# A decoder layer on one core: PSUM banks chosen per job and tile at the two ends, another order of all work, and a quarter of the last experts' sums on ScalarE

## The reference

```python
# 1 causal self-attention, 16 heads of 8, polymax in place of a softmax
q, k, v = split(x @ W_attn, 3)
att = where(causal, q @ k.T / sqrt(8), -inf)
att = where(att > 0, att**2 + 1, where(att >= -100, -0.01 * att + 1, 0)) / 1000
x = layernorm(x + (att @ v) @ W_proj)
# 2 cross-attention, 16 heads of 64
q, k, v = x @ WQ, ctx @ WK, ctx @ WV
x = layernorm(x + softmax(q @ k.T / 8) @ v @ WO + bO)
# 3 16 experts, the 6 best kept by a router
probs = softmax(x @ router_w.T + router_b)
gate = top 6 of probs / (their sum + 1e-10), 0 elsewhere
out = sum over e of gate[:, e] * (x @ expert_w[e])
x = layernorm(x + out / max(sum(gate), 1e-10) + 1e-10 * sum(top_p))
```

## Time and profile before

| | |
|---|---|
| median of three runs | 1014.57 us (1012.44 to 1014.77) |
| profiled execution: its own time | 1011.26 us |
| its span, first to last instruction | 1009.5 us |
| mean granted clock of TensorE | 0.986 |
| PE busy | 955.2 us, 95% |
| PEld busy | 843.0 us, 84% |
| DVE busy | 890.6 us, 88% |
| ACT busy | 768.7 us, 76% |
| POOL busy | 434.3 us, 43% |
| instructions | 47204 |

### The profile page before, as it was taken

The page is one execution under the profiler, slowest core; times in us unless marked ns, Lnnn a source line. Parts: engine busy times, 40 slices in busy tenths (PEclk is TensorE's granted clock), DMA queues, the critical chain, the costliest instruction groups (busy, mean ns, idle before and its releaser), DMA issues.

```text
span 1009.5 us, 47204 instructions
## 1 busy us (share of the span) xinstructions
PE 955.2 (95%) x18136; PEld 843.0 (84%) x18136; DVE 890.6 (88%) x2824; ACT 768.7 (76%) x1606; POOL 434.3 (43%) x906
## 2 busy tenths in 40 slices
...
DMA packets 41882, 21.19 MB, mean 21 GB/s; under 512 B 18912, under 2 KB 40928, under 8 KB 41824
## 3 DMA queue, kind: packets, MB, share of 16 engines
...
...
## 4 chain that ended last, share of the span: by engine, by line
PE 66%; DVE 17%; issue 11%; ACT 3%; DVEq 1%; POOL 1%; DMA 0%; ACTq 0%; SPq 0%; POOLq 0%
PE ps L447 61%; DVE sums L888 4%; PE ps L572 4%; DVE allowed L852 3%; DVE p L864 2%; DVE stats L805 1%; DVE residual L888 1%; ACT prob L764 1%; DVE mv L811 1%; DVE best L911 1%; PE ps L595 1%; DVE ps L859 1%; DVEq L354 0%; ACT qm L636 0%; DVE left L920 0%
## 5 line engine op out<-in xcount | busy, mean ns | idle before, releaser
L888 DVE SCALAR_TENSOR_TENSOR sums<-ps,gate,sums 128x128 f32<-128x128 f32 x896 | 239.9, 340 | 18.5 <-PE ps L447 17.7
L996 POOL TENSOR_TENSOR p<-p,rowinv 128x1024 f32<-128x1024 f32 x64 | 121.8, 1904 | 219.1 <-DVE rowinv L841 219.0
L447 PE MATMUL ps<-wo_sb,oT 128*128 128x128 f32 x1024 | 127.5, 278 | 0.6 <-issue 0.6
L447 PEld LDWEIGHTS ps<-wo_sb,oT 128*128 128x128 f32 x1024 | 121.1, 192 | 5.4 <-issue 1.0
L636 ACT ACTIVATE v<-ps 128x512 f32<-128x512 f32 x128 | 76.3, 598 | 50.2 <-PE ps L447 45.2
L447 PE MATMUL ps<-ex_hi,x2T_hi 128*128 128x512 f32 x256 | 110.4, 431 | 3.3 <-POOL x2T_lo L978 3.1
L636 ACT ACTIVATE oT<-ps 128x512 f32<-128x512 f32 x128 | 69.6, 597 | 45.7 <-PE ps L447 45.1
L756 ACT ACTIVATE x<-residual,shift,rstd 128x128 f32<-128x128 f32 x192 | 83.7, 484 | 26.9 <-POOL shift L991 17.5
L447 PE MATMUL ps<-ex_lo,x2T_hi 128*128 128x512 f32 x256 | 101.7, 397 | 0.0
L447 PE MATMUL ps<-ex_hi,x2T_lo 128*128 128x512 f32 x256 | 101.5, 396 | 0.0
L852 DVE SCALAR_TENSOR_TENSOR allowed<-ps,const 128x512 f32<-128x512 f32 x128 | 87.1, 681 | 15.2 <-ACT relu L659 13.6
...
## 6 DMA issues: line engine op xcount, KB each, us to landing
...
```

The source lines that it names most:

```text
L447: return pe.matmul(o, l, r, start=start, stop=stop)
L888: done = V.scalar_tensor_tensor(after, ps(f"FF{4 * r + q}")[:, C * e:C * e + C], gate[:, r, 4 * q + e:4 * q + e + 1], before, ALU.mult, AL ...
L996: G.tensor_tensor(weights, weights, rowinv[:, r].unsqueeze(2).broadcast_to([P, H, T]), ALU.mult).then_inc(p2_ready, 1)
```

## The change

The diff does six things.

- `OTHER_BANK_FIRST` and `OTHER_BANK_LAST` name, for 205 entries of job and tile in head and tail, a bank other than that of `JOBS`. `banks_of` and `ps` take the tile.
- `JOBS` and `ORDER` hold another order and other banks for the loop. The turns run from 1 to 26, with a turn touching tiles from t - 1 to t + 4; FF3 and FF7 stand at t - 1.
- Head and tail orders are new. heads1, heads2 and heads0 take the pairs P3, P2 and P0, in this order, the first two right behind S1 of tile 0. `x_columns@2` stands ahead of `x_rows@1` on SP, `queries@1` ahead of `square3@0` on ACT.
- w_attn and the constants are issued on ACT's queue; on SP the order is WK, ctx of tile 0, WV, WQ.
- Four matmuls (`WARM`) on a tile of zeros run before PE's first wait.
- For the last three tiles (`SHARED`) `weigh3` is replaced. `scale3` on ACT multiplies the eight products of quarter 3 with their gates into SBUF, `gather3` on POOL adds them to one sum in two additions, and `join3` on DVE adds that to `sums`.

```diff
...
+SHARED = 3
+WARM = 4
...
+    ("FF7", "B0", -1), ("K2_0", "B1", 2), ("X2T", "B7", 0), ("PT0b", "B6", 1), ("Q", "B3", 4),
+    ("FF3", "B4", -1), ("K", "B5", 4), ("V", "B2", 4), ("Y", "B1", 3), ("S2_0", "P3", 2),
+    ("AC0", "P2", 1), ("S2_1", "P0", 2), ("LG", "B3", 0), ("PT1a", "B5", 1), ("PR", "B2", 3),
+    ("S1_0", "B7", 4), ("PT1b", "B3", 1), ("S1_1", "B4", 4), ("V2_0", "B5", 2), ("S1_2", "B6", 4),
+    ("S1_3", "B3", 4), ("AC1", "P0", 1), ("WO0", "B2", 1), ("WO1", "", 1), ("FF1", "B0", 0),
+    ("V2_3", "B1", 2), ("V2_1", "B7", 2), ("V2_2", "B2", 2), ("FF6", "B4", 0), ("PT0a", "B5", 2),
+    ("X1T", "B7", 3), ("FF4", "B1", 0), ("FF0", "B2", 0), ("Q2_0", "B7", 3), ("Q2_1", "B6", 3),
+    ("FF5", "B5", 0), ("FF2", "B3", 0), ("K2_1", "B7", 3), ("K2_3", "B6", 3), ("Q2_2", "B1", 3),
+    ("Q2_3", "B7", 3), ("K2_2", "B2", 3), ("heads0", "P0", None), ("heads1", "P0", None), ("heads2", "P0", None),
...
+        store@-1 context@4 x_rows@4 x_columns@5
...
+        mK2_3@2 mK2_0@2 mK2_2@2 mX2T@0 mPT0b@1 queries@4 kK@4 mV@4 mY@3 mAC0@1 norm3@-1 mPT1a@1 mPT1b@1 exp0@2 logit_exp@0 relu0@4
+        mV2_0@2 mAC1@1 relu1@4 square0@4 square1@4 relu2@4 square2@4 relu3@4 mV2_3@2 norm1@3 mV2_1@2 mV2_2@2 square3@4 x1_hi@3
+        mPT0a@2 exp1@2 base3@0 mQ2_0@3 mQ2_1@3 mK2_1@3 norm2@1 mQ2_2@3 mQ2_3@3
...
+        row_sum1@1 row_inv1@1 weigh3@-1 stats3@-1 var3@-1 row_max0@2 less_max0@2 logits@0 row_max1@2 less_max1@2 gate0@0 projected@3
+        row_sum0@2 row_inv0@2 gate1@0 stats1@3 var1@3 allow0@4 allow1@4 pieces0@4 gate2@0 pieces1@4 gate3@0 p1_0@4 gate4@0 attended@1
+        gate5@0 gate6@0 p1_1@4 allow2@4 gate7@0 gate8@0 stats2@1 allow3@4 gate9@0 pieces2@4 gate10@0 x1_lo@3 p1_2@4 var2@1 pieces3@4
+        p1_3@4 weigh0@0 weigh1@0 weigh2@0
...
+        next_x_hi@4 next_x_lo@4 shares1@1 x2_hi@0 root3@-1 x2_lo@0 shares0@2 root1@3 bias_x1@2 gshare0@0 gshare1@0 gshare2@0
+        context_hi@3 gshare3@0 gshare4@0 gshare5@0 gshare6@0 root2@1 context_lo@3
...
-FIRST_TURN, LAST_TURN = 1, NT - 7
...
+OTHER_BANK_FIRST = """
+    Q@0=B6 Q@1=B7 Q@2=B7 Q@3=B5 Q@4=B7 K@0=B2 K@1=B6 K@2=B1 K@3=B1 K@4=B7 V@0=B7 V@1=B5 V@3=B1 V@4=B0 S1_0@0=B1 S1_0@1=B6
...
+    PT0b@1=B0 AC0@1=P3 S2_1@0=P3 S2_1@2=P2 PT1a@0=B0 PT1a@1=B4 PT1b@0=B7 PT1b@1=B6 AC1@0=P2 AC1@1=P3 WO0@0=B5 X2T@0=B6 LG@0=B7
+    FF0@0=B1 FF4@0=B7 FF1@0=B5 FF5@0=B6 FF2@0=B0 heads1@0=P3 heads2@0=P2
...
+OTHER_BANK_LAST = """
+    K@-1=B2 V@-1=B3 S1_0@-1=B5 S1_1@-1=B2 S1_2@-1=B7 S1_3@-1=B4 Y@-2=B6 Y@-1=B5 PR@-2=B6 PR@-1=B4 X1T@-2=B2 X1T@-1=B1 Q2_0@-2=B1
...
+FIRST_TURN, LAST_TURN = 1, NT - 6
...
-        x_columns@1 context@1 x_rows@1 x_columns@2 x_columns@3 x_columns@4 x_rows@2 context@2 x_columns@5 x_rows@3 x_columns@6
-        x_rows@4 context@3 x_rows@5 context@4
+        x_columns@1 context@1 x_columns@2 x_rows@1 x_columns@3 x_columns@4 x_rows@2 context@2 x_rows@3 context@3 context@4 x_rows@4
+        x_columns@5
...
+        K@0 Q@0 V@0 S1_0@0 S1_1@0 S1_2@0 S1_3@0 heads1@0 heads2@0 K@1 Q@1 heads0@0 V@1 S1_0@1 S1_1@1 Y@0 S1_2@1 S1_3@1 PR@0 Q@2 K@2
+        V@2 K2_0@0 K2_2@0 K2_3@0 X1T@0 K2_1@0 S1_0@2 S1_1@2 S1_2@2 S1_3@2 Q@3 Q2_1@0 Y@1 V2_1@0 Q2_0@0 V2_0@0 K@3 Q2_3@0 PR@1 Q2_2@0
+        V@3 S2_0@0 V2_2@0 V2_3@0 S2_1@0 X1T@1 K2_0@1 K2_1@1 K2_2@1 S1_0@3 S1_1@3 S1_2@3 S1_3@3 Q@4 Q2_0@1 K2_3@1 Y@2 Q2_2@1 PT0b@0
...
+        kK@0 queries@0 mV@0 relu0@0 square0@0 relu1@0 heads_hi1@0 square1@0 relu2@0 square2@0 heads_hi2@0 relu3@0 queries@1 square3@0
+        heads_hi0@0 kK@1 experts_hi@0 mY@0 mV@1 relu0@1 relu1@1 square0@1 queries@2 kK@2 square1@1 relu2@1 norm1@0 square2@1 mK2_0@0
+        x1_hi@0 mK2_3@0 relu3@1 mK2_2@0 square3@1 mK2_1@0 relu0@2 queries@3 square0@2 relu1@2 mQ2_1@0 mY@1 square1@2 relu2@2 mV2_1@0
...
+        mPT0b@-1 norm3@-5 mPT0a@-1 mPT1a@-1 mPT1b@-1 base3@-3 scale3@-3 norm2@-2 mAC0@-1 mX2T@-2 mAC1@-1 logit_exp@-2 norm3@-4
+        base3@-2 scale3@-2 norm2@-1 mX2T@-1 norm3@-3 logit_exp@-1 base3@-1 scale3@-1 norm3@-2 norm3@-1
...
+        weigh1@-3 var3@-4 logits@-2 gate0@-2 weigh2@-3 gate1@-2 gate2@-2 join3@-3 gate3@-2 gate4@-2 gate5@-2 gate6@-2 gate7@-2
+        attended@-1 gate8@-2 stats3@-3 gate9@-2 stats2@-1 gate10@-2 var3@-3 var2@-1 weigh0@-2 weigh1@-2 weigh2@-2 logits@-1 gate0@-1
+        join3@-2 gate1@-1 gate2@-1 gate3@-1 gate4@-1 gate5@-1 gate6@-1 gate7@-1 gate8@-1 gate9@-1 stats3@-2 var3@-2 gate10@-1
+        weigh0@-1 weigh1@-1 weigh2@-1 join3@-1 stats3@-1 var3@-1
...
+        gshare4@-3 gshare5@-3 gshare6@-3 root2@-2 gather3@-3 root3@-4 x2_hi@-2 x2_lo@-2 gshare0@-2 gshare1@-2 gshare2@-2 gshare3@-2
...
+def banks_at(words, base=0):
+    return {(job, base + int(tile)): bank for job, tile, bank in (word.replace("=", "@").split("@") for word in words.split())}
...
-def banks_of(job):
-    return {"": (), "P": (2 * int(BANK[job][1:] or 0), 2 * int(BANK[job][1:] or 0) + 1), "B": (int(BANK[job][1:] or 0),)}[BANK[job][:1]]
+def banks_of(job, tile):
+    bank = OTHER_BANK.get((job, tile), BANK[job]) if isinstance(tile, int) else BANK[job]
+    n = int(bank[1:] or 0)
+    return {"": (), "P": (2 * n, 2 * n + 1), "B": (n,)}[bank[:1]]
...
+        def shared_index(tile):
+            return tile - (NT - SHARED) if isinstance(tile, int) else -1
+        def wait_summed(eng, tile):
+            if shared_index(tile) >= 0:
+                eng.wait_ge(joined, shared_index(tile) + 1)
+                for job in ("FF3", "FF7"):
+                    wait_emptied(eng, job, tile)
...
-            sp.dma_start(w_attn_sb[:], w_attn).then_inc(attn_in, 16)
-            sp.dma_start(const[:], consts).then_inc(const_in, 16)
-            for dst, src, arrived in zip(heads_ld, (wq_t, wk_t, wv_t), heads_in):
-                sp.dma_start(dst, src).then_inc(arrived, 16)
+            sp.dma_start(heads_ld[1], wk_t).then_inc(heads_in[1], 16)
             load(cT, ctx_t, cT_in, 0)
+            sp.dma_start(heads_ld[2], wv_t).then_inc(heads_in[2], 16)
+            sp.dma_start(heads_ld[0], wq_t).then_inc(heads_in[0], 16)
...
+            pe.wait_ge(zeroed, 1)
+            rows_of_zeros = vp[:].rearrange("p b g n -> p (b g n)")
+            for _ in range(WARM):
+                mm(pairs[0][:, 0:P], rows_of_zeros[:, 0:P], rows_of_zeros[:, 0:P])
             pe.wait_ge(attn_split, 1)
...
+            nc.scalar.dma_start(w_attn_sb[:], w_attn).then_inc(attn_in, 16)
+            nc.scalar.dma_start(const[:], consts).then_inc(const_in, 16)
             act.wait_ge(attn_in, 16)
...
+            def scale_last(tile, q):
+                act.wait_ge(share_steps, SHARE_STEPS * (tile + 1))
+                wait(act, extra_ready, shared_index(tile))
+                for r in range(NR):
+                    wait_full(act, f"FF{4 * r + q}", tile)
+                    for e in range(4):
+                        last = nc.scalar.activation(scaled_out[:, r, e], ps(f"FF{4 * r + q}", tile)[:, C * e:C * e + C], ACT.Copy, scale=gate[:, r, 4 * q + e:4 * q + e + 1])
+                    last.then_inc(emptied[f"FF{4 * r + q}"], 1)
...
+            def join(tile, q):
+                dve.wait_ge(extra_ready, shared_index(tile) + 1)
+                for r in range(NR):
+                    wait_emptied(dve, f"FF{4 * r + q - 1}", tile)
+                wait(dve, normed[3], tile)
+                V.tensor_tensor(residual[3][:], sums[:], extra[:], ALU.add).then_inc(joined, 1)
...
+            def gather(tile, q):
+                for r in range(NR):
+                    wait_emptied(pool, f"FF{4 * r + q}", tile)
+                wait(pool, joined, shared_index(tile))
+                G.tensor_tensor(scaled_out[:, :, 0:2], scaled_out[:, :, 0:2], scaled_out[:, :, 2:4], ALU.add).then_inc(halves_added, 1)
+                pool.wait_ge(halves_added, shared_index(tile) + 1)
+                G.tensor_tensor(extra[:], scaled_out[:, :, 0], scaled_out[:, :, 1], ALU.add).then_inc(extra_ready, 1)
...
```

More of the change, by code:

```diff
@@ L93 @@
-        S2_0@2 Q@5 AC0@1 S2_1@2 V2_1@2 PT1b@1 V2_3@2 AC1@1 WO0@1 V2_2@2 S1_0@5 V2_0@2 S1_1@5 S1_2@5 S1_3@5 K2_2@3 K2_0@3 WO1@1 K2_1@3
-        PT0b@2 PR@4 X2T@0 K2_3@3 LG@0 X1T@3 PT0a@2 PT1a@2 PT1b@2 Q2_0@3 Q2_2@3 Q2_3@3 Q2_1@3 FF5@0 FF0@0 FF4@0 AC0@2 Q@6 FF1@0 AC1@2
-        S2_0@3 V2_1@3 K@6 V2_2@3 S2_1@3 WO0@2 WO1@2 FF6@0 FF2@0 Y@5 V@6 X2T@1 FF7@0 FF3@0
+        K@0 Q@0 V@0 S1_0@0 S1_1@0 S1_2@0 S1_3@0 heads1@0 heads2@0 K@1 Q@1 heads0@0 V@1 S1_0@1 S1_1@1 Y@0 S1_2@1 S1_3@1 PR@0 Q@2 K@2
+        V@2 K2_0@0 K2_2@0 K2_3@0 X1T@0 K2_1@0 S1_0@2 S1_1@2 S1_2@2 S1_3@2 Q@3 Q2_1@0 Y@1 V2_1@0 Q2_0@0 V2_0@0 K@3 Q2_3@0 PR@1 Q2_2@0
@@ new lines @@
+        V@3 S2_0@0 V2_2@0 V2_3@0 S2_1@0 X1T@1 K2_0@1 K2_1@1 K2_2@1 S1_0@3 S1_1@3 S1_2@3 S1_3@3 Q@4 Q2_0@1 K2_3@1 Y@2 Q2_2@1 PT0b@0
+        Q2_1@1 Q2_3@1 PT0a@0 PT1a@0 PT1b@0 AC0@0 S2_0@1 V2_0@1 K@4 AC1@0 V2_1@1 S2_1@1 PR@2 WO0@0 V2_3@1 V2_2@1 WO1@0 S1_0@4 K2_3@2
+        S1_1@4 K2_1@2 S1_2@4 S1_3@4 Y@3 X1T@2 K2_0@2 K2_2@2 PT0b@1 PR@3 PT0a@1 Q2_3@2 Q2_2@2 AC0@1 V2_1@2 Q2_1@2 Q2_0@2 V2_0@2 WO0@1
```

(6 more changed lines are left out.)

271 lines of the change are left out of this document (133 added, 138 removed), and 9 rows, old and new, of the table JOBS.

## The result

The changed kernel takes 978.70 us (median of four runs, 976.82 to 980.67), the kernel before 1014.67 (1012.44 to 1016.00). The ratio is 0.9648, 95% interval 0.9621 to 0.9675. The profiled execution took 977.77 us with a span of 975.5, where before it was 1011.26 and 1009.5: the span is 34.0 us shorter. The sum of the prediction put that execution at 993.0.

The account below looks back on a forecast made before the run. The prediction took PE to fill the loop, with 51 us idle at the two ends. Fill -12.3, drain -6.0 and loop 0 made -18.3 us: 993.0 on the profiled execution, 996 us on the median, range 984 to 1009.

Parts of the forecast that it names:

- The loop: Steady turns: the new order leaves the turn at 29.27 us, gain 0, with -8 to +8 us over 26 turns.
- 0.2 of runs: Loop: four runs of fp32r jobs instead of five save PE 0.2 us a turn.
- dearer neighbours: Loop, inside fp32 runs: WO0 directly ahead of WO1 and Y ahead of S2_0 cost more, against the 0.2 us saved.
- The fourth rival: Loop closes up to PE's own 29.0 us a turn: -7 us, so 989; chance 0.12.
- The first rival: Loop gets longer, hanging on a close wait: at 0.9 us a turn, 1019 us; chance 0.14.
- the close waits: Loop: FF2 for S1_3's bank, Q2_0 for x1_lo, K2_1@3 for context_lo@3; inputs 0 to 0.6 us ahead of use.
- The fill: Start up to the loop: earlier loads and less idle give -12.3 us, between -3 and -21.
- the 1.2 for the runs: Head: fp32r runs fall from 29 to 23, -1.2 us.
- The second rival: Fill wins little, as x of tile 1 and queries@1 ahead of square3@0 delay it: -3 us, so 1005; chance 0.18.
- The drain: End after the loop: experts' share, fewer fp32r runs and less idle give -6.0 us, between -1 and -9.
- that of the last tile: Drain, last tile: ACT's share of the experts' sums ends the last sum 0.8 us earlier.
- The third rival: Drain wins nothing: join waits for POOL, norm2 behind scale3, DVE waits as long as it saved; 1002 us; chance 0.10.

Follow-up runs that it names:

- light DVE: Kernel before with half of the experts' weighted sums cut to 16 of 128 columns: turn 29.06 us; the same cut in the changed kernel: 28.57 us.
- the run with FF0 first: Kernel before with FF0 moved ahead of PT1a, PT0b and PT1b: 1054.69 us, ratio 1.0428, turn 31.03 us.

## Why the prediction was half right

**The loop** is the step that failed: "I take 29.27, that is 0, with -0.3 to +0.3 us a turn". The turn is 28.57, -0.69 from 29.26. The parts: 0.20 us were waits of PE for DVE (shown by light DVE, where the prediction saw 0.13 of idle and "a little in PT1a"), and 0.16 a wait of Q for x (shown by the traces and by the run with FF0 first), which the prediction had nowhere for the old turn. That leaves 0.33 for PE's order, for which the prediction had 0.2 of runs, given back by dearer neighbours. A run costs 0.31 in the one place of the new loop where it was added, so it can be nearly all of the rest; but removing another would have saved 0.06. Job by job the rest is on balance 0.2 in fp32r jobs, as in FF0, FF3 and V2_1, which cost 0.09 to 0.10 less, and 0.1 in fp32 jobs, where the neighbours that I feared were dearer (AC1 by 0.16) and others cheaper (AC0 by 0.28). That the runs did it is argued and not shown for the old loop. The fourth rival, the loop that closes up to PE's own time, is what happened, with -15 instead of its -7, because PE's own time in the new order was put at 29.0 to 29.15.

**The first rival** did not come, but its condition was near: each job that I moved in either loop to another place, save K, ended at one of the close waits, on ACT, on a bank, or on DVE, and the turn grew by 0.4 to 1.8 us.

**The fill** was right in its sum, -13.0 for -12.3, and in its mechanism: X1T@0 at 34.55 for 34, Y@0 1.8 us later for 2. The sum is partly luck. By the pricing above the loss falls by 3.9 us up to relu0 of tile 2 (forecast 3.6), by 7.1 from there to relu0 of tile 4 (4.3), and by 2.0 after that, where 3.2 and most of the 1.2 for the runs were put. The largest part is the load of x for tile 2 (4.4 to 5.8 us up to S1 of tile 2); the load order gives 1.4 at K@1, the zeros 0. The second rival's wait is there, ACT stands 4.14 us at `queries@1`, but costs less than it, since the chain goes through the load of x for tile 1.

**The drain** was right in sum, -5.6 for -6.0; of its terms only that of the last tile was measured alone. The share gives 1.5 us there for the forecast 0.8. The forecast had `join` wait for `extra`, with FF3 done 2.0 to 2.8 us behind the first sum and 2.9 us of products. ACT begins 0.35 us behind the first sum and takes 2.17, so that `extra` is ready at 967.82 and DVE's own sums end at 969.38: `join` waits for those alone, and the share is worth eight products less one `join`. The third rival is refuted for the last tile. The Trainium skill, "ScalarE: Activation LUTs", section "Rules for kernel authors", speaks for the multiplication on VectorE; here ACT takes 0.27 us a product and DVE 0.26, so it is no slower to speak of, and the measurement decides for the share where DVE bounds the stage and ACT idles.
